# A vision tower with experts on one core: seven tiles embedded in the first turns, logits spread out, norm statistics on ScalarE

## The chip, the cores and the metric

One NeuronCore of one Trainium2 chip. The metric is the device time of one execution in microseconds; lower is better. The change is compared with the kernel before by the medians of several executions.

## What is computed

32 images of 3 x 96 x 96 become 36 patches each plus a class token: 1184 rows of 256 numbers, in ten tiles of 128 rows (the last has 32). Then:

```python
h = embed(x)                                  # patches @ W.T + b, class token, positions
x0 = layernorm(h)                             # no weights
xn = layernorm(x0) * w1 + b1
q, k, v = xn @ Wq.T, xn @ Wk.T, xn @ Wv.T     # + biases; 16 heads of 16
q, k = elu(q) + 1, elu(k) + 1
attn = per token, over its heads: q (k v) / (q sum(k))
x1 = x0 + attn @ Wo.T + bo
x2 = layernorm(x1) * w2 + b2
h2 = h + x1 + gelu(x2 @ Wfc.T + bfc) @ Wproj.T + bproj
y = layernorm(h2)                             # no weights
scores = softmax(y @ gate.T)                  # 16 experts, each takes its 148 best rows
out = h2 + shared_mlp(y) + sum over the chosen experts of weight * expert(y)
```

All in float32; the attention works within one token, so tiles are independent until the experts choose their rows.

## The kernel before

Five engines run written-out streams that meet by semaphores; nothing schedules them but the order of the code. The front half is a software pipeline of ten turns (`turn(t)` on TensorE, ScalarE and VectorE, a loop of the same shape on GpSimd). In turn t the tiles stand at different stages: tile t has its attention products made on VectorE, tile t-1 is summed by transposes (`sum_values`), projected and normed to x2, tile t-2 goes through the hidden layer (`mlp`, `project_mlp`), tile t-3 is normed to y and turned, tile t+1 is projected to q, k, v, tile t+2 is normed (x0, xh) and turned, and tile t+3 is embedded (`embed`, seven matmuls) at the end of the turn.

- Norms: VectorE makes mean and variance of 256 numbers with two instructions (`moments`, L777 and L780), three times a tile: `a_moments` of h, `c_moments` of x1, `f_moments` of h2. GpSimd turns them into 1/sqrt and a shift (`inverse_root`, `shift_of`), ScalarE applies these (`norm_a`, `scale_xh`, `norm_c`, `norm_f`; L550, L570). xh is x0 with its second norm's factor.
- ScalarE also copies PSUM to SBUF (`copy_h`, `copy_v`, `turn_attn`, `turn_y`), and has Exp in the same turn as Gelu, which have different tables (ACT_TABLE_LOAD). `load_exp` loads the table of Exp early with a tiny activation on `warm`.
- Embedding has one PSUM bank and two patch buffers: TensorE waits until the last tile's copy was made, SyncE asks for the patches of tile n as soon as tile n-2 was embedded. Small matmuls without use (`keep_busy`) fill TensorE's first waits.
- Behind the last turns a tail finishes tiles 8 and 9. The seven first of 20 blocks of the shared MLP's first layer are made in and behind turns 8 and 9 (`EARLY`), the others and the second layer are a filler between the steps of the routing (`fill`). The logits of tiles 0 to 8 come at once before the last tile's y is turned:

```python
turn_y(s9.off(-1))
early(5, 6)
pe.wait_ge(yT_made, TILES - 1)
for t in range(TILES - 1):
    logits(t)
turn_y(s9)
```

- Then come softmax, ten rounds of counting that find each expert's threshold (VectorE and TensorE in turn), the slots, and from about 305 us on sixteen experts, which the change does not touch.

## Time and profile before

| | us |
|---|---|
| median of 3 executions | 504.08 (502.46 to 504.34) |
| profiled execution, its own time | 504.55 |
| its span, first to last instruction | 502.8 |
| TensorE busy | 459.9 (91%) |
| VectorE busy | 362.0 (72%) |
| ScalarE busy | 224.4 (45%) |
| GpSimd busy | 152.3 (30%) |
| chain that ended last: PE, DVE, ACT, issue | 66%, 14%, 5%, 5% |

In rows, PE is TensorE (its matmuls; weight loads have rows of their own), DVE VectorE, ACT ScalarE, POOL GpSimd. L followed by a number is a line of the kernel. A bracket at a timeline's row tells how long the engine was idle before it, and what released it. A float32 matmul counts as two. Shares of busy time are averages over all stages: what an engine costs is read in a turn.

### The profile page before, as it was taken

The page shows a single profiled execution, that of the slowest core. Times are in us where ns is not written, and L with a number is a line of the kernel's source. Part 1 is how long each engine was busy: PE and PEld are TensorE (multiplying, and loading weights), DVE is VectorE, ACT ScalarE, POOL GpSimd, SP SyncE. Part 2 cuts the span into 40 slices and gives each one's busy share as a digit, 9 for nine tenths or more (in the row PEclk, how much of TensorE's full clock was granted, in tenths as well). Part 3 has the DMA queues.
Part 4 walks back from the last instruction along what each step waited for, and adds up shares of the span by engine and source line. Part 5 has one row for each costly group of instructions (what it writes and reads, how often), then busy time and mean ns, then how long its engine had stood idle before and what let it go on. Part 6 is the DMA issues. An engine that isn't in the chain of part 4 may idle for free.

```text
span 502.8 us, 10363 instructions
## 1 busy us (share of the span) xinstructions
PE 459.9 (91%) x3853; PEld 404.9 (81%) x3853; DVE 362.0 (72%) x674; ACT 224.4 (45%) x527; POOL 152.3 (30%) x252
## 2 busy tenths in 40 slices
PE   6987899999999998999798499899999999999990
PEld 3555778888888887888677388899999999999990
DVE  1289898999999999621488687588877667777720
ACT  1432264664664752334341005445555566666520
POOL 1312033142142122121000052164433747446322
PEclk9999699999999999999789969989999999999996
DMA  7965101101000000000000016978878888888421
GB/s 246 370 231 252 35 1 34 43 1 45 10 13 0 12 12 10 1 10 23 7 1 0 0 29 220 372 275 303 295 286 284 307 324 329 319 319 324 113 26 13
DMA packets 17348, 69.12 MB, mean 137 GB/s; under 512 B 4338, under 2 KB 10399, under 8 KB 12834
## 3 DMA queue, kind: packets, MB, share of 16 engines
q1 hardware_dynamic: 12130, 61.96, 32.9%
q0 software_dynamic: 4608, 5.41, 5.3%
q10 hardware_dynamic: 576, 1.29, 0.7%
q8 instruction: 22, 0.36, 0.3%
q14 instruction: 12, 0.10, 0.1%
HBM read 63.32 MB, written 5.33 MB: 137 GB/s over the span
## 4 chain that ended last, share of the span: by engine, by line
PE 66%; DVE 14%; ACT 5%; issue 5%; DMA 3%; POOL 1%; DVEq 0%; ACTq 0%; POOLq 0%
PE bank L1407 18%; PE bank L1418 13%; PE bank L1181 5%; PE bank L1210 5%; PE bank L1195 5%; PE bank L1125 4%; PE bank L1315 4%; DVE qkt L795 4%; DMA wex_s<-in_wex 3%; DVE scratch L961 2%; PE bank L1140 2%; DVE scratch L790 2%; PE bank L1169 1%; DVE late L809 1%; PE bank L1429 1%
## 5 line engine op out<-in xcount | busy, mean ns | idle before, releaser
L1418 PE MATMUL bank<-scratch,wex_s 128*128 128x148 f32 x512 | 78.4, 297 | 0.2 <-DVE scratch L1053 0.2
L503 POOL DMA_INDIRECT out_rows<-scratch,slot_s x32 | 51.8, 1619 | 83.9 <-DMA out_rows<-scratch,slot_s 61.5
L492 POOL DMA_INDIRECT xg<-token_rows,slot_g x32 | 44.5, 1391 | 81.2 <-DVE slot_g L1026 72.3
L1418 PEld LDWEIGHTS bank<-scratch,wex_s 128*128 128x128 f32 x512 | 68.2, 192 | 0.5 <-DVE scratch L1053 0.5
L420 POOL TENSOR_SCALAR tmp<-mv 128x1 f32<-128x1 f32 x30 | 6.7, 222 | 166.6 <-DVE mv L780 166.6
L724 ACT ACTIVATE scratch<-bank 128x296 f32<-128x296 f32 x64 | 26.6, 416 | 67.2 <-PE bank L1407 67.2
L1407 PE MATMUL bank<-scratch,wsh_s 128*128 128x148 f16 x512 | 53.7, 230 | 0.0
L1407 PE MATMUL bank<-scratch,wfc_s 128*128 128x148 f16 x512 | 52.6, 228 | 0.0
L1407 PE MATMUL bank<-scratch,wproj_s 128*128 128x148 f16 x256 | 50.6, 227 | 0.0
L944 DVE SCALAR_TENSOR_TENSOR wproj_s<-wex_s,wfc_s 128x512 f16<-128x512 f32 x64 | 40.4, 682 | 12.6 <-ACT wfc_s L707 12.6
L1053 DVE SCALAR_TENSOR_TENSOR scratch<-bank,scratch 128x296 f32<-128x296 f32 x64 | 29.4, 460 | 27.0 <-ACT scratch L724 26.9
L790 DVE TENSOR_TENSOR scratch<-qk 128x2048 f32<-128x2048 f32 x20 | 45.5, 2291 | 4.2 <-PE bank L1195 3.9
L795 DVE TENSOR_REDUCE qkt<-scratch 128x128 f32<-128x2048 f32 x20 | 45.1, 2257 | 0.3 <-issue 0.3
L1407 PEld LDWEIGHTS bank<-scratch,wsh_s 128*128 128x128 f16 x512 | 42.9, 99 | 1.2
L1407 PEld LDWEIGHTS bank<-scratch,wfc_s 128*128 128x128 f16 x512 | 42.1, 98 | 1.5 <-issue 0.4
L1169 PEld LDWEIGHTS bank<-x2T,wfc_s 128*128 128x128 f32 x320 | 37.2, 192 | 4.4 <-issue 3.3
L1407 PE MATMUL bank<-scratch,wtok_s 128*128 128x148 f16 x192 | 40.0, 230 | 0.0
L1210 PE MATMUL bank<-yT,wsh_s 128*128 128x256 f32 (+1 forms) x160 | 38.3, 396 | 0.0
L707 ACT ACTIVATE wfc_s<-wex_s 128x512 f16<-128x512 f32 x64 | 36.5, 632 | 3.6 <-DMA wex_s<-in_wex 3.6
L1169 PE MATMUL bank<-x2T,wfc_s 128*128 128x128 f32 x320 | 37.5, 276 | 0.7 <-ACT x2T L574 0.7
L1181 PE MATMUL bank<-wproj_s,hidT 128*128 128x256 f32 x160 | 36.9, 384 | 0.8
L944 DVE SCALAR_TENSOR_TENSOR wtok_s<-wex_s,wsh_s 128x512 f16<-128x512 f32 x48 | 30.2, 682 | 8.9 <-ACT wsh_s L707 8.9
(162 smaller groups left out, 908.0 us busy)
## 6 DMA issues: line engine op xcount, KB each, us to landing
wex_s<-in_wex SPq DMA_DIRECT2D x16, 2048.0 KB, 7.9
wex_s<-in_wex SPq DMA_DIRECT2D x16, 1024.0 KB, 8.4
patch_s<-in_patches SPq DMA_DIRECT2D x10, 384.0 KB
token_rows<-y_s SPq DMA_DIRECT2D x10, 128.0 KB, 1.8
out_rows<-h_all SPq DMA_DIRECT2D x5, 256.0 KB, 6.5
wfc_s<-in_wfc SPq DMA_DIRECT2D x1, 1024.0 KB, 5.2
wproj_s<-in_wproj SPq DMA_DIRECT2D x1, 1024.0 KB, 7.2
wsh_s<-in_wsh SPq DMA_DIRECT2D x1, 1024.0 KB, 8.9
```

The lines of the kernel that those rows point to most:

```text
L492: gp.indirect_dma_start(xg[b][:], None, rows, bass.IndirectOffsetOnAxis(slot_g[b][:], 0))\
L503: gp.indirect_dma_start(out, bass.IndirectOffsetOnAxis(slot_s[b][:], 0), eo[b], None, compute_op=ALU.add).then_inc(scattered, 16)
L707: act.activation(w16(s.par, 0, n), wex_s[s.par][:, n * n16:(n + 1) * n16], ACT.Copy, scale=SPLIT).then_inc(whi_made, 1)
L790: ve.tensor_tensor(dst.rearrange("p (h j d) -> p h j d", h=HH, j=H), q, k, ALU.mult).then_inc(v_chain, 1)
L795: ve.tensor_reduce(qkt[:, g * HH:(g + 1) * HH, :], src.rearrange("p (h j d) -> p h j d", h=HH, j=H), AX, ALU.add).then_inc(v_chain, 1)
L944: ve.scalar_tensor_tensor(w16(s.par, 1, n), wex_s[s.par][:, n * n16:(n + 1) * n16], SPLIT, w16(s.par, 0, n), ALU.mult, ALU.subtract).then_ ...
L1053: ve.scalar_tensor_tensor(hexT[:, 2 * p:2 * p + 2, :].rearrange("p m c -> p (m c)"), ps_up[p % 2][:, 0:2 * C], 1 / SPLIT ** 2, gel[p % 2], ...
L1169: last = pe.matmul(ps_fc[m // 4][:, (m % 4) * P:(m % 4 + 1) * P], wfc_s[:, k, m * P:(m + 1) * P], x2T[:, k, :], start=(k == 0), stop=(k == ...
L1181: last = pe.matmul(ps_proj[:, 0:D], hidT[:, m, :], wproj_s[:, m, :], start=False, stop=(m == MC - 1))
L1210: last = pe.matmul(ps_shared(j)[:, x * SPAN:x * SPAN + width(lo)], wsh_s[:, k, x * SH + m * P:x * SH + (m + 1) * P], yT[:, k, lo:lo + widt ...
L1407: last = pe.matmul(dst[p % 2][:, x * C:(x + 1) * C], w16(s.par, a, piece)[:, lo:lo + P], x16[s.par][b][:, k, :], start=(n == 0), stop=(n = ...
L1418: last = pe.matmul(ps_down[k][:, 0:C], wex_s[s.par][:, lo:lo + P], hexT[:, m, :], start=(m == 0), stop=(m == MC - 1))
```

## The change

1. The tiles are embedded earlier: tiles 2 and 3 ahead of turn 0 (in the place of 14 idle matmuls), 4, 5, 6 in turn 0, 7 and 8 in turn 1, 9 in turn 2. The odd ones use bank 7, the others bank 0. The loads of patches move ahead of those of the hidden layer, the shared MLP and the experts; the stores of y move behind all loads.
2. The logits of tile t-4 come in turn t, the last three in the tail. One shared block less is made early (six).
3. `moments` goes. The copy of the embedding and the two additions give the row's sum beside their result (`accum_out`; the additions become scalar_tensor_tensor). ScalarE makes minus the mean of it (`less`), then a Square with that as its bias, whose own running sum is 256 times the variance (`spread`). GpSimd scales this sum, and needs one instruction less for the shift.

```diff
-        ps_tok, ps_tr, ps_qk, ps_v, ps_o = bank[0], bank[1], bank[2], bank[3], bank[4]
+        ps_tr, ps_qk, ps_v, ps_o = bank[1], bank[2], bank[3], bank[4]
         ps_fc, ps_proj = (bank[5], bank[6]), bank[7]
...
+        def ps_tok(t):
+
+            return bank[7 if t % 2 and t < TILES - 1 else 0]
...
-        stats = sb("stats", [P, 3, 6])
-        mv = sb("mv", [P, 3, 2])
-        tmp = sb("tmp", [P, 9])
+        total, less, spread = sb("total", [P, 3, TILES]), sb("less", [P, 3, TILES]), sb("spread", [P, 3, TILES])
+        beside = sb("beside", [P, D])
+        tmp = sb("tmp", [P, 6])
...
-        EARLY = 7
+        EARLY = 6
...
-            sp.dma_start(wo_s[:], wo).then_inc(w_in["o"], 16)
-            sp.dma_start(wfc_s[:], wfc).then_inc(w_in["fc"], 16)
-            sp.dma_start(wproj_s[:], wproj).then_inc(w_in["proj"], 16)
...
             next_patch(Step(0, 2))
+            sp.dma_start(wo_s[:], wo).then_inc(w_in["o"], 16)
+            next_patch(Step(0, 3))
+            sp.dma_start(wfc_s[:], wfc).then_inc(w_in["fc"], 16)
+            sp.dma_start(wproj_s[:], wproj).then_inc(w_in["proj"], 16)
+            for t in range(4, TILES):
+                next_patch(Step(0, t))
             sp.dma_start(gate_s[:], gate).then_inc(w_in["moe"], 16)
             sp.dma_start(wsh_s[:], wsh).then_inc(w_in["moe"], 16)
             sp.dma_start(wsd_s[:], wsd).then_inc(w_in["moe"], 16)
-            next_patch(Step(0, 3))
-            next_patch(Step(0, 4))
             load_gu(Step(0, 0), 0)
             load_dn(Step(0, 0), 0)
             load_gu(Step(0, 1), 1)
-            for t in range(5, TILES):
-                next_patch(Step(0, t))
-                if t >= 8:
-                    store_y(Step(0, t - 8))
-            for t in range(TILES - 8, TILES):
+            for t in range(TILES):
                 store_y(Step(0, t))
...
-            def inverse_root(k, var, base_count):
+            def inverse_root(k, squares, base_count):
 
                 gp.sem_inc(p_passed, 1)
-                gp.tensor_scalar(tmp[:, k:k + 1], var, EPS, None, ALU.add).then_inc(p_chain, 1)
+                gp.tensor_scalar(tmp[:, k:k + 1], squares, 1 / D, EPS, ALU.mult, ALU.add).then_inc(p_chain, 1)
                 gp.wait_ge(p_chain, base_count(1))
                 return gp.tensor_tensor(rstd[:, k:k + 1], tmp[:, k:k + 1], nhalf[:], ALU.pow)
 
-            def shift_of(k, at):
+            def shift_of(k, t, at):
 
                 gp.wait_ge(p_chain, at(2))
-                gp.tensor_tensor(tmp[:, 6 + k:7 + k], rstd[:, k:k + 1], mv[:, k, 0:1], ALU.mult).then_inc(p_chain, 1)
-                gp.wait_ge(p_chain, at(3))
-                return gp.tensor_tensor(shift[:, k:k + 1], tmp[:, 6 + k:7 + k], minus[:], ALU.mult)
+                return gp.tensor_tensor(shift[:, k:k + 1], rstd[:, k:k + 1], less[:, k, t:t + 1], ALU.mult)
...
+            def squares(k, t, src, done):
+
+                nonlocal means
+                means += 1
+                act.sem_inc(a_passed, 1)
+                act.activation(less[:, k, t:t + 1], total[:, k, t:t + 1], ACT.Copy, scale=-1 / D).then_inc(mean_made, 1)
+                act.wait_ge(mean_made, means)
+                act.sem_inc(a_passed, 1)
+                act.activation(beside[:], src, ACT.Square, bias=less[:, k, t:t + 1],
+                               accum_out=spread[:, k, t:t + 1]).then_inc(done, 1)
+
             def copy_h(s):
                 act.wait_ge(tok_done, s.times(1, 1))
-                act.activation(h_all[:, s.n, :], ps_tok[:, 0:D], ACT.Copy).then_inc(h_copied, 1)
+                act.activation(h_all[:, s.n, :], ps_tok(s.n)[:, 0:D], ACT.Copy, accum_out=total[:, 0, s.n:s.n + 1]).then_inc(h_copied, 1)
+                act.wait_ge(h_copied, s.times(1, 1))
+                squares(0, s.n, h_all[:, s.n, :], a_stats)
+
+            def squares_c(s):
+                act.wait_ge(x1_made, s.times(1, 1))
+                squares(1, s.n, x_all[:, s.n, :], c_stats)
+
+            def squares_f(s):
+                act.wait_ge(h2_made, s.times(1, 1))
+                squares(2, s.n, h_all[:, s.n, :], f_stats)
...
+            copy_h(Step(0, 2))
             turn_xn(Step(0, 1))
+            copy_h(Step(0, 3))
...
-            def turn(t, blocks=()):
+            def turn(t, soon=(), late_on=(), blocks=()):
                 s = Step(0, t)
                 if t + 1 < TILES:
                     load_exp()
...
                     copy_v(s.off(1))
                     negate_qk(s.off(1))
                     exp_qk(s.off(1))
+                if t >= 3:
+                    squares_f(s.off(-3))
                 if t >= 2:
                     gelu(s.off(-2))
+                if t >= 1:
+                    squares_c(s.off(-1))
                 if t + 2 < TILES:
                     norm_a(s.off(2))
                     scale_xh(s.off(2))
+                for n in soon:
+                    copy_h(Step(0, n))
                 if t >= 3:
                     norm_f(s.off(-3), t >= 5)
                 if t >= 1:
...
                     turn_xn(s.off(2))
                 if t >= 3:
                     turn_y(s.off(-3))
-                if t + 3 < TILES:
-                    copy_h(s.off(3))
+                for n in late_on:
+                    copy_h(Step(0, n))
                 for j in blocks:
                     gelu_shared(j)
 
-            for t in range(TILES - 2):
+            turn(0, (4,), (5, 6))
+            turn(1, (7,), (8,))
+            turn(2, (), (9,))
+            for t in range(3, TILES - 2):
                 turn(t)
-            turn(TILES - 2, (0,))
-            turn(TILES - 1, (1, 2))
+            turn(TILES - 2, blocks=(0,))
+            turn(TILES - 1, blocks=(1, 2))
...
             gelu(s9.off(-1))
+            squares_f(s9.off(-2))
             turn_attn(s9)
             gelu_shared(3)
             norm_f(s9.off(-2))
+            squares_c(s9)
             norm_c(s9)
             turn_x2(s9)
             turn_y(s9.off(-2))
+            squares_f(s9.off(-1))
             gelu_shared(4)
             gelu(s9)
             norm_f(s9.off(-1))
             turn_y(s9.off(-1))
+            squares_f(s9)
             gelu_shared(5)
             norm_f(s9)
-            gelu_shared(6)
             load_exp()
             turn_y(s9)
...
-            def a_moments(s, at):
-                ve.wait_ge(h_copied, s.times(1, 1))
-                ve.wait_ge(a_rstd, s.times(1, 0))
-                moments(0, h_all[:, s.n, :], at, a_stats)
-
-            def c_moments(s, at):
+            def add_attn(s):
                 ve.wait_ge(o_done, s.times(1, 1))
                 ve.wait_ge(x0_made, s.times(1, 1))
-                ve.tensor_tensor(x_all[:, s.n, :], ps_o[:, 0:D], x_all[:, s.n, :], ALU.add).then_inc(x1_made, 1)
-                ve.wait_ge(x1_made, s.times(1, 1))
-                ve.wait_ge(c_rstd, s.times(1, 0))
-                moments(1, x_all[:, s.n, :], at, c_stats)
-
-            def f_moments(s, at):
+                ve.scalar_tensor_tensor(x_all[:, s.n, :], ps_o[:, 0:D], 1.0, x_all[:, s.n, :], ALU.mult, ALU.add,
+                                        accum_out=total[:, 1, s.n:s.n + 1]).then_inc(x1_made, 1)
+
+            def add_mlp(s):
                 ve.wait_ge(proj_done, s.times(1, 1))
                 ve.wait_ge(hx_made, s.times(1, 1))
-                ve.tensor_tensor(h_all[:, s.n, :], ps_proj[:, 0:D], hx[:], ALU.add).then_inc(h2_made, 1)
-                ve.wait_ge(h2_made, s.times(1, 1))
-                ve.wait_ge(f_rstd, s.times(1, 0))
-                moments(2, h_all[:, s.n, :], at, f_stats)
+                ve.scalar_tensor_tensor(h_all[:, s.n, :], ps_proj[:, 0:D], 1.0, hx[:], ALU.mult, ALU.add,
+                                        accum_out=total[:, 2, s.n:s.n + 1]).then_inc(h2_made, 1)
 
             def combine(s):
...
-                if t + 2 < TILES:
-                    a_moments(s.off(2), after(1))
                 if t >= 3:
-                    f_moments(s.off(-3), after(1))
+                    add_mlp(s.off(-3))
                 qk_sum(s, 1, mine, product1)
                 after(1)
                 if t >= 1:
-                    c_moments(s.off(-1), after(1))
+                    add_attn(s.off(-1))
                 for j in blocks:
...
+            def embed(t):
+
+                s = Step(0, t)
+                pe.wait_ge(patch_in[s.par], s.half * 32 + 32)
+                if t >= 2:
+                    pe.wait_ge(h_copied, t - 1 if t < TILES - 1 else t)
+                pe.matmul(ps_tok(t)[:, 0:D], sel_s[s.par][:], base_s[:], start=True, stop=False)
+                for k in range(TKC):
+                    last = pe.matmul(ps_tok(t)[:, 0:D], patch_s[s.par][:, k, :], wtok_s[:, k, :], start=False, stop=(k == TKC - 1))
+                last.then_inc(tok_done, 1)
...
-            keep_busy(10)
+            embed(2)
             turn_xh(Step(0, 1))
-            keep_busy(4)
-
-            embed(Step(0, 2))
-
-            def turn(t, blocks=()):
+            embed(3)
+
+            def turn(t, soon=(), late_on=(), blocks=()):
...
+                for n in soon:
+                    embed(n)
                 if t >= 1:
                     turn_x2(s.off(-1))
                 if t + 2 < TILES:
                     turn_xh(s.off(2))
                 if t >= 3:
                     turn_y(s.off(-3))
-                if t + 3 < TILES:
-                    embed(s.off(3))
+                if t >= 4:
+                    logits(t - 4)
+                for n in late_on:
...
-            turn(0)
+            turn(0, (4,), (5, 6))
             pe.wait_ge(w_in["o"], 16)
-            turn(1)
+            turn(1, (7,), (8,))
             pe.wait_ge(w_in["fc"], 16)
             pe.wait_ge(w_in["proj"], 16)
-            for t in range(2, TILES - 2):
+            turn(2, (), (9,))
+            turn(3)
+            pe.wait_ge(w_in["moe"], 48)
+            pe.wait_ge(h_copied, TILES)
+            for t in range(4, TILES - 2):
                 turn(t)
-            pe.wait_ge(w_in["moe"], 48)
-            turn(TILES - 2, (0,))
-            turn(TILES - 1, (1, 2))
+            turn(TILES - 2, blocks=(0,))
+            turn(TILES - 1, blocks=(1, 2))
...
             project_mlp(s9.off(-1))
+            logits(TILES - 4)
             early(4)
             turn_x2(s9)
             turn_y(s9.off(-2))
...
             project_mlp(s9)
             pe.wait_ge(yT_made, TILES - 2)
             turn_y(s9.off(-1))
-            early(5, 6)
+            logits(TILES - 3)
+            early(5)
             pe.wait_ge(yT_made, TILES - 1)
-            for t in range(TILES - 1):
-                logits(t)
+            logits(TILES - 2)
             turn_y(s9)
             pe.wait_ge(yT_made, TILES)
             logits(TILES - 1).then_inc(logits_done, 1)
```

Three places show how the order moves. ScalarE, a whole turn in the middle, before (`warm` starts the turn; neg and expo are the Exp of tile t+1, hidT the Gelu of tile t-2):

```order
L597 ACTIVATE attnT<-bank 128x256
L593 ACTIVATE vx<-bank 128x256
L585 ACTIVATE neg<-bank 128x512
L589 ACTIVATE expo<-neg 128x512
L608 ACT_TABLE_LOAD
L608 ACTIVATE hidT<-bank,colc 128x128 x8
L550 ACTIVATE x_all<-h_all,shift,rstd 128x256
L570 ACTIVATE xh<-x_all,rstd 128x256
L550 ACTIVATE y_s<-h_all,shift,rstd 128x256
L550 ACTIVATE x<-x_all,shift,rstd 128x256
L574 ACTIVATE x2T<-bank,colc 128x128 x2
L574 ACTIVATE xnT<-bank,colc 128x128 x2
```

and now, the same place:

```order
L615 ACTIVATE vx<-bank 128x256
L607 ACTIVATE neg<-bank 128x512
L611 ACTIVATE expo<-neg 128x512
L550 ACTIVATE less<-total 128x1
L553 ACTIVATE beside,spread<-h_all,less 128x256
L630 ACT_TABLE_LOAD
L630 ACTIVATE hidT<-bank,colc 128x128 x8
L550 ACTIVATE less<-total 128x1
L553 ACTIVATE beside,spread<-x_all,less 128x256
L572 ACTIVATE x_all<-h_all,shift,rstd 128x256
L592 ACTIVATE xh<-x_all,rstd 128x256
L572 ACTIVATE y_s<-h_all,shift,rstd 128x256
```

One pair of less and beside (the squares of h2) stands between expo and the Gelu table load, a second (those of x1) between hidT and the norms.

TensorE up to the first sum of values (L1195), before from the transpose of xh of tile 1 (L1110):

```order
L1110 MATMUL bank<-kst,xh 128x128 x2
L1232 MATMUL bank<-ones_b 128x512 x4
L1123 MATMUL bank<-base_s,sel_s 128x256
L1125 MATMUL bank<-wtok_s,patch_s 128x256 x6
L1114 MATMUL bank<-bias_s,ones_b 128x256
L1147 MATMUL bank<-wqkv_s,xnT 128x256 x2
L1114 MATMUL bank<-bias_s,ones_b 128x512
L1140 MATMUL bank<-wqkv_s,xnT 128x512 x2
L1110 MATMUL bank<-kst,xh 128x128 x2
L1123 MATMUL bank<-base_s,sel_s 128x256
L1125 MATMUL bank<-wtok_s,patch_s 128x256 x6
L1195 MATMUL bank<-kst,scratch 128x128 x16
```

and now from the projections of tile 1:

```order
L1126 MATMUL bank<-bias_s,ones_b 128x256
L1157 MATMUL bank<-wqkv_s,xnT 128x256 x2
L1126 MATMUL bank<-bias_s,ones_b 128x512
L1150 MATMUL bank<-wqkv_s,xnT 128x512 x2
L1134 MATMUL bank<-base_s,sel_s 128x256
L1136 MATMUL bank<-wtok_s,patch_s 128x256 x6
L1122 MATMUL bank<-kst,xh 128x128 x2
L1134 MATMUL bank<-base_s,sel_s 128x256
L1136 MATMUL bank<-wtok_s,patch_s 128x256 x6
L1134 MATMUL bank<-base_s,sel_s 128x256
L1136 MATMUL bank<-wtok_s,patch_s 128x256 x6
L1205 MATMUL bank<-kst,scratch 128x128 x16
```

The embeddings of tiles 2 and 3 now stand ahead of the first row. Before the first sum of values the tiles up to 6 are embedded, where it was up to 3.

TensorE's tail, from the last projection of the hidden layer (L1181), before:

```order
L1181 MATMUL bank<-wproj_s,hidT 128x256 x8
L1110 MATMUL bank<-kst,y_s 128x128 x2
L1210 MATMUL bank<-yT,wsh_s 128x256 x8
L1219 MATMUL bank<-gate_s,yT 128x16 x18
L1110 MATMUL bank<-kst,y_s 128x128 x2
L1219 MATMUL bank<-gate_s,yT 128x16 x2
```

and now:

```order
L1191 MATMUL bank<-wproj_s,hidT 128x256 x8
L1122 MATMUL bank<-kst,y_s 128x128 x2
L1229 MATMUL bank<-gate_s,yT 128x16 x2
L1220 MATMUL bank<-yT,wsh_s 128x256 x4
L1229 MATMUL bank<-gate_s,yT 128x16 x2
L1122 MATMUL bank<-kst,y_s 128x128 x2
L1229 MATMUL bank<-gate_s,yT 128x16 x2
```

The 18 logit matmuls before the last turned y have become 2 and 2, and one shared block of four is gone from between.

## Rows read from the trace of the kernel before

**Rows 1.** Chain that ended last: start (us), length (us), engine and line.

```profile
78.37 3.49 PE bank L1195 x32
...
174.54 2.28 DVE scratch L790
...
192.34 2.29 DVE scratch L790
```

**Rows 2.** Timeline, turn 5: start, busy us, engine, line, operation, out<-in.

```profile
106.04 1.28 ACT L608 ACT_TABLE_LOAD   x1
...
108.53 3.72 PE L1181 MATMUL bank<-wproj_s,hidT 128*128 128x256 f32 x16
...
109.35 0.64 ACT L550 ACTIVATE x_all<-h_all,shift,rstd 128x256 f32<-128x256 f32 x1
...
111.01 0.58 ACT L550 ACTIVATE x<-x_all,shift,rstd 128x256 f32<-128x256 f32 x1
...
112.09 0.38 PE L1110 MATMUL bank<-kst,x 128*128 128x128 f32 x2
```

**Rows 3.** Timeline of TensorE, turn 7 (the first that embeds nothing).

```profile
154.10 1.91 PE L1195 MATMUL bank<-kst,scratch 128*128 128x128 f32 x16
...
169.01 0.38 PE L1110 MATMUL bank<-kst,x 128*128 128x128 f32 x2
...
170.34 1.94 PE L1195 MATMUL bank<-kst,scratch 128*128 128x128 f32 x16 [0.51 <-issue]
```

**Rows 4.** Timeline of VectorE, statistics of turn 7; idle time before in brackets.

```profile
158.26 0.42 DVE L777 BATCH_NORM_STATS2 stats<-h_all 128x6 f32<-128x256 f32 x1
...
158.93 0.43 DVE L827 TENSOR_TENSOR h_all<-bank,hx 128x256 f32<-128x256 f32 x1
159.53 0.43 DVE L777 BATCH_NORM_STATS2 stats<-h_all 128x6 f32<-128x256 f32 x1 [0.17 <-DVE h_all L827]
```

**Rows 5.** Groups by line and form, 0 to 270 us: busy us, mean ns of one.

```profile
L570 ACT ACTIVATE xh<-x_all,rstd 128x256 f32<-128x256 f32 x10 | 5.1, 508 | 2.3 <-POOL rstd L422 1.4
...
L535 ACT ACTIVATE warm<-warm 1x1 f32<-1x1 f32 x11 | 2.2, 198 | 0.1
...
L961 DVE DVE_READ_ACCUMULATOR scratch<-scratch,way 128x1 f32 x7 | 0.6, 83 | 0.0
```

**Rows 6.** Timeline, first turns, all engines, 0 to 60 us.

```profile
25.70 2.86 PE L1125 MATMUL bank<-wtok_s,patch_s 128*128 128x256 f32 x12
...
33.93 0.44 PE L1110 MATMUL bank<-kst,xh 128*128 128x128 f32 x2 [2.46 <-ACT xh L570]
...
34.92 4.54 PE L1125 MATMUL bank<-wtok_s,patch_s 128*128 128x256 f32 x12
...
39.30 1.91 PE L1195 MATMUL bank<-kst,scratch 128*128 128x128 f32 x16
...
51.70 0.69 PE L1110 MATMUL bank<-kst,x 128*128 128x128 f32 x2 [4.85 <-ACT x L550]
...
59.17 2.19 PE L1195 MATMUL bank<-kst,scratch 128*128 128x128 f32 x16
```

**Rows 7.** Timeline, the last turns and the tail, all engines, 188 to 244 us.

```profile
201.73 0.44 PE L1110 MATMUL bank<-kst,x 128*128 128x128 f32 x2 [1.45 <-ACT x L550]
...
230.13 3.62 PE L1210 MATMUL bank<-yT,wsh_s 128*128 128x256 f32 x16
...
233.24 0.60 ACT L550 ACTIVATE y_s<-h_all,shift,rstd 128x256 f32<-128x256 f32 x1 [0.80 <-POOL shift L429]
...
233.59 4.38 PE L1219 MATMUL bank<-gate_s,yT 128*128 128x16 f32 x36
...
238.94 1.03 PE L1219 MATMUL bank<-gate_s,yT 128*128 128x16 f32 x4 [0.47 <-ACT yT L614]
```

**Rows 8.** Timeline, TensorE at the stage that finds the slots.

```profile
288.60 1.40 PE L1366 MATMUL bank<-late 128*74 128x4 bf16 x20 [5.24 <-DVE late L1013]
```

**Rows 9.** Page: granted TensorE clock in tenths, 40 slices of 12.57 us.

```profile
PEclk9999699999999999999789969989999999999996
```

More of the change, by code:

```diff
@@ L451, in norm_f @@
                 gp.wait_ge(y_made, s.times(1, 0))
[L452 to L453 removed]
+                inverse_root(2, spread[:, 2, s.n:s.n + 1], at).then_inc(p_chain, 1)
+                shift_of(2, s.n, at).then_inc(f_rstd, 1)
             def sum_hx(s):
@@ L468, in after @@
                 return lambda k: base + k
-            norm_a(Step(0, 0), after(6))
-            norm_a(Step(0, 1), after(6))
+            norm_a(Step(0, 0), after(5))
+            norm_a(Step(0, 1), after(5))
             for t in range(TILES + 3):
@@ L474, in _ @@
                 if t + 2 < TILES:
-                    norm_a(s.off(2), after(6))
+                    norm_a(s.off(2), after(5))
                 if t >= 3:
-                    norm_f(s.off(-3), after(3))
+                    norm_f(s.off(-3), after(2))
                 if 2 <= t < TILES + 2:
@@ L480, in _ @@
                 if 1 <= t <= TILES:
-                    norm_c(s.off(-1), after(3))
+                    norm_c(s.off(-1), after(2))
             def gather(s, first):
@@ L846, in shared_hidden @@
                                  gel_sh[:, (j % 2) * SPAN:(j % 2) * SPAN + n], ALU.mult).then_inc(shid_made, 1)
-            chain = 2
+            chain = 0
             def after(n):
@@ L900, in _ @@
             shared_hidden(1)
-            f_moments(s9.off(-2), after(1))
+            add_mlp(s9.off(-2))
             shared_hidden(2)
-            c_moments(s9, after(1))
+            add_attn(s9)
             shared_hidden(3)
-            f_moments(s9.off(-1), after(1))
+            add_mlp(s9.off(-1))
             shared_hidden(4)
-            f_moments(s9, after(1))
+            add_mlp(s9)
             shared_hidden(5)
-            shared_hidden(6)
             def link(ins):
@@ L1114, in add_bias @@
                 pe.matmul(dst[:, 0:n], ones_b[0:BP, :], bias_s[:, lo:lo + n], start=True, stop=False)
-            def embed(s, part=None):
-                cut = TKC // 2
-                if part != 1:
-                    pe.wait_ge(patch_in[s.par], s.half * 32 + 32)
-                    if not (isinstance(s.n, int) and s.n == 0):
-                        pe.wait_ge(h_copied, s.times(1, 0))
-                    pe.matmul(ps_tok[:, 0:D], sel_s[s.par][:], base_s[:], start=True, stop=False)
-                for k in range(cut if part == 1 else 0, cut if part == 0 else TKC):
-                    last = pe.matmul(ps_tok[:, 0:D], patch_s[s.par][:, k, :], wtok_s[:, k, :], start=False, stop=(k == TKC - 1))
-                if part != 0:
-                    last.then_inc(tok_done, 1)
+            def embed(t):
[7 more added lines that the diff above has]
+                last.then_inc(tok_done, 1)
             def turn_xh(s):
@@ L1236, in _ @@
             pe.wait_ge(w_in["tok"], 32)
-            embed(Step(0, 0))
-            embed(Step(0, 1))
+            embed(0)
+            embed(1)
             pe.wait_ge(w_in["consts"], 32)
```

30 lines of the change are left out of this document (10 added, 20 removed).

## The prediction

> **What bounds the kernel now.** I read the chain of waits first. From 78 to 154 us it is a TensorE chain: the transposes that sum one tile's values start at 78.37 and, four turns later, at 154.10, so a turn takes 18.93 us [rows 1, 3]. In turns 8 and 9 the chain runs through VectorE, with 17.80 us from product to product [rows 1]. The change acts on exactly these two engines. The timeline of one TensorE-bound turn shows what else lies close: after the exponentials ScalarE loads the Gelu table at 106.04, TensorE can start projecting the hidden layer only at 108.53, and the normalised x2 starts at 111.01, lasts 0.58 and is turned by TensorE at 112.09, some 0.44 us later than it could have been [rows 2]. The reader should see that ScalarE is only half busy and still has almost no slack at two places in a turn. Turn 7, which embeds nothing, shows TensorE's turn without an embedding: 154.10 to 170.34, 16.24 us. Its last piece, from turning x2 (169.01) to the next sum, is 1.33 us, which waits for ScalarE to write x2T [rows 3]. The last view is the tail, where 36 narrow logit matmuls hold TensorE for 4.38 us between the last tile's norm and its transpose [rows 7].
>
> **What changes, part by part.**
>
> *VectorE.* Each pair of statistics instructions goes: 158.26 to 158.93, 0.67 us, and behind the two additions also a 0.17 us wait for their own result [rows 4]. That is 3 x 0.67 + 2 x 0.17 = 2.35 us a turn. The additions become forms with a running sum; the only accumulator read in the trace costs 0.08 [rows 5], so 0.16 comes back. VectorE's full turn, 18.5 (17.80 for turn 8, which lacks one pair, plus 0.67), falls to about 16.3. So VectorE leaves the bound. By itself this gains nothing in the turns that TensorE bounds.
>
> *ScalarE.* Each pair comes back there as a mean (one element per partition) and a Square over 256. The nearest rows are 0.198 for the tiny activation and 0.508 for a 256-wide one with one per-partition operand [rows 5]. With two gaps of 0.03 that is 0.77. Reading the sum out is in no row of ScalarE: lower bound nothing (0.77, or 0.71 if the gaps overlap), upper bound another full activation (1.3). I take 0.1, near VectorE's 0.08, so s = 0.87 for one pair.
>  Square is not used before, so a table could have to be loaded for it. A load is 1.28 us [rows 2]; two more a turn would cost six turns some 15 us. The order of instructions has 16 loads before and 16 after, so I add none. [...]
>
> *TensorE, steady turns.* Tiles 5 to 9 are no longer embedded in turns 2 to 6 (only tile 9 stays, in turn 2). The turn falls from 18.93 to 16.24, and the 0.49 us of logits that is added (4.38/9, [rows 7]) fits into the 1.33 us at its end: turn xh and turn y take 0.4 of that. But the f pair now stands between the exponentials and the Gelu table load, on the path to 108.53, at full price: +0.87. The c pair stands between Gelu and the x2 norm: +0.87 less the 0.44 of slack, +0.43. Its other path, through GpSimd, is the same length or shorter: the three norms ahead of x2 take 1.66 (109.35 to 111.01). New turn: 16.24 + 0.87 + 0.43 = 17.54. From the sum of tile 2 to that of tile 7 there are five: 87.7 against 92.0 (78.37 to 170.34). **-4.3.**
>
> *First turns.* Seven embeddings (2 and 3 ahead, 4 to 6 in turn 0, 7 and 8 in turn 1, 9 in turn 2) at 2.86 x 7/6 = 3.3 us each at full clock [rows 6] replace four. Copying tile 1 now also squares it, ahead of the first xnT: +0.6. The count, in full clock: tile 0's projections end at about 21.9; embedding 2 to 25.2, xh of tile 1 to 25.6, embedding 3 to 28.9, projections of tile 1 (2.9) to 31.8, embeddings 4, 5, 6 and a turned xh to 42.1, so tile 0 is summed 2.8 us later than now (39.30). From a sum to x2 a turn takes 14.9 (154.10 to 169.01, [rows 3]), 7.5 of it the hidden layer, which turn 1 lacks: 42.1 + 7.4 = 49.5, embedding 7 to 52.8. Today TensorE then sits idle for 4.85 us at 51.70 for x2, and sums tile 1 at 59.17 with a slow clock [rows 6]. After the change x2 comes at about 54.9, since it queues on ScalarE behind the copy and squares of tile 7: 2.1 us idle, two transposes, embedding 8, and tile 1 is summed at 58.6 (VectorE has it ready at about 57). Turn 2: 58.6 + 14.9 + 0.4 of stall + 0.4 + 3.3 = 77.6, against 78.37. The patches have two buffers; each is asked for two embeddings ahead, and weights are moved behind them, so I charge no wait for data. [...] -0.8 + 1.7 = **+0.9.**
>
> *Turn 8.* It embeds nothing before either, and gains an obstacle: 16.24 - 1.33 + 0.4 (two transposes) + 0.5 (logits) + 1.8 (a shared block, half of 3.62, [rows 7]) = 17.65, plus 0.87 + 0.3 for the pairs = 18.8 on TensorE, against 17.8 on VectorE now. **+1.0.**
>
> *Turn 9.* TensorE waited 1.45 us for x2 [rows 7]. VectorE reaches that addition 0.84 sooner, the squares cost 0.2 more than the statistics, GpSimd has one instruction less (0.27). **-0.8.**
>
> *Tail.* Logits 5 and 6 come before the last projection: **+1.0.** After it, the last norm now starts at about 233.2, as at 233.24 today (squares 0.1 to 0.2 dearer, GpSimd one instruction less). Today TensorE turns it only at 238 (233.59 + 4.38), after one more shared block and nine logits; now it is free at 232.9 (230.13 + 1.8 + 2 x 0.49). What is late next is ScalarE: norm to 233.8, table load and warm-up to 235.3, yT to 235.7, then the last logits, 0.5 to 1.0, to 236.5, against 239.97 [rows 7]. **-3.5.**
>
> *Middle.* The seventh shared block (1.8 us) moves into the filler behind the routing rounds. There TensorE is idle for 5.24 us [rows 8] and six more filler matmuls go into that gap, so the block is hidden; without that cover it costs 1.8. Behind this gap the slice from 289 to 302 us shows a granted clock of 6 tenths [rows 9], so most of four filler groups of 1.8 us ran twice as long. A gap of 2.6 instead of 5.24 should shorten that. Bounds: nothing, and 3.8 us; I take **-1.0.** The expert phase is not touched.
>
> Sum: -4.3 + 0.9 + 1.0 - 0.8 + 1.0 - 3.5 - 1.0 = -6.7. The profiled execution took 504.55 and so gives 497.85; it lies 0.47 over the median shown (504.08), and against that median I forecast **497.4 us**.
>
> **The rivals.**
> 1. *ScalarE becomes the bound (slower).* The place is the f pair between exp and Gelu and the c pair behind Gelu. Every 0.1 us of s costs twice in six turns and once or twice at both ends, 1.4 us. [...] At s = 1.6 the time is 497.4 + 7.3 x 1.4 = 507.6. For it: no accumulating activation in the trace. Against it: the cheap 0.08 of VectorE's. Chance 0.13. [...]
> 2. *The opening gives it back (no change).* The half clock lasts as after the 4.85 us gap (+2.3), a second dip comes in turn 0 (+1.7) and a patch is 1 us late: 502.4. For it: the clock fell at both places today [rows 6, 9]. Against: TensorE has more work there, not less. Chance 0.13.
> 3. *The pairs are hidden and VectorE bounds every turn.* Five turns at 16.34 in place of 17.54 and turn 8 at 17.7: 6.0 + 1.1 less, 490.3. For it: ScalarE is half idle. Against it: [rows 2] show no slack at the hidden layer. Chance 0.08.
>
> **How the numbers follow.** My forecast has 0.66 and spreads from 494 (s = 0.71, no dip in the clock) to 502 (s = 1.1, a longer dip). Within 0.5% is about what a measurement of this kernel can tell from no change, that is 501.6 to 506.6. Faster by more than that: 0.62 of my own case, 0.04 of the second rival, 0.08 of the third, 0.74. Within: 0.04 + 0.09 + 0.02 of the first, 0.15. Slower: the rest of the first rival, 0.11. The range 492.5 to 505 leaves out most of rivals 1 and 3, 0.19 together.
>
> **What would show it.** In the profile after: turns 3 to 7 of 17.5 us between sums of values; a gap of about 1 us on TensorE before the hidden projection and of 0.4 before x2 is turned; Square near 0.5 and the pair near 0.87; VectorE with over 1 us idle a turn; tile 2 summed between 77 and 80; scores starting 3.5 us sooner behind the last projection; a shorter half-clock stretch in the slot stage. I am wrong if the pair takes over 1.3 us (then slower), if turns come out at 16.3 (then rival 3), or if tile 2 is summed after 82 (rival 2).

## Result: 8.6% slower, where 1.3% faster was forecast

| | before | changed |
|---|---|---|
| median of 4 executions, us | 503.27 (500.52 to 504.34) | 545.78 (544.86 to 547.46) |
| ratio, 95% interval | | 1.086 (1.082 to 1.090) |
| span of the profiled execution | 502.8 | 543.2 |
| TensorE, VectorE, ScalarE, GpSimd busy | 459.9, 362.0, 224.4, 152.3 | 468.9, 345.6, 248.2, 204.1 |
| mean granted TensorE clock | 0.953 | 0.935 |

GpSimd is the surprise: one instruction less a norm, and 52 us more busy. From the page of the changed kernel: the clock row, to compare with [rows 9], the chain's shares, and a group of two-operand scalar instructions on 128 single numbers.

```profile
PEclk9999798978989788798998988998999999999996
...
PE 58%; POOL 10%; DVE 5%; ACT 4%; issue 4%; DMA 2%; POOLq 0%; ACTq 0%; DVEq 0%
...
L421 POOL TENSOR_SCALAR tmp<-spread 128x1 f32<-128x1 f32 x30 | 24.9, 829 | 167.7 <-ACT beside L553 163.1
```

Before, GpSimd had 1% of the chain (the chain of waits that ended last), and now 10%. The mean of 829 ns hides two kinds. The view of one line gives minimum, median and maximum in ns; first the 1/sqrt of the changed kernel, then the same line before.

```profile
L423 POOL TENSOR_TENSOR rstd<-tmp,nhalf x40: 549/550/2670, 13.8 to 279.6; 128x1 f32<-128x1 f32 x40
```

```profile
L422 POOL TENSOR_TENSOR rstd<-tmp,nhalf x40: 567/568/576, 13.6 to 232.0; 128x1 f32<-128x1 f32 x40
```

The median is as it was; some take five times as long. Timeline of one turn of the changed kernel, GpSimd, VectorE and what waits (start, busy us; idle time before in brackets):

```profile
122.05 0.21 POOL L421 TENSOR_SCALAR tmp<-spread 128x1 f32<-128x1 f32 x1 [12.04 <-ACT beside L553]
122.31 2.29 DVE L835 TENSOR_TENSOR scratch<-qkt,vx 128x2048 f32<-128x2048 f32 x1
...
122.34 2.67 POOL L423 TENSOR_TENSOR rstd<-tmp,nhalf 128x1 f32<-128x1 f32 x1
...
124.52 2.29 DVE L835 TENSOR_TENSOR late<-qkt,vx 128x2048 f32<-128x2048 f32 x1
125.09 1.77 POOL L428 TENSOR_TENSOR shift<-rstd,less 128x1 f32<-128x1 f32 x1
...
125.95 0.18 ACT L553 ACTIVATION_READ_ACCUMULATOR beside<-x_all,less 128x1 f32 x1
...
127.44 2.29 DVE L816 TENSOR_TENSOR scratch<-qk 128x2048 f32<-128x2048 f32 x1
127.62 2.15 POOL L421 TENSOR_SCALAR tmp<-spread 128x1 f32<-128x1 f32 x1
...
129.86 0.55 POOL L423 TENSOR_TENSOR rstd<-tmp,nhalf 128x1 f32<-128x1 f32 x1
130.49 0.19 POOL L428 TENSOR_TENSOR shift<-rstd,less 128x1 f32<-128x1 f32 x1
...
130.80 0.60 ACT L572 ACTIVATE x<-x_all,shift,rstd 128x256 f32<-128x256 f32 x1 [3.07 <-POOL shift L428]
...
131.45 0.67 PE L1122 MATMUL bank<-kst,x 128*128 128x128 f32 x2 [3.40 <-ACT x L572]
```

The second L421 starts 0.18 us behind a product of 2.29 us and ends at 129.77, 0.04 behind the product's end at 129.73; L423 (122.34) ends 0.41 behind its product, about its own length. So a tiny instruction that meets a product seems to do its work only when the product has ended: in the trace of the changed kernel 29 GpSimd instructions start while such a product runs, and every one of them ends behind it: by 0.05 us those that otherwise take 0.19, by 0.41 those that take 0.55, by 0.59 those that take 0.73. Both operands of these products (L816, L835) lie in SBUF. The norm of x2 is late twice over. GpSimd takes y's norm first, which meets two products (L423 at 122.34, L428 at 125.09); it comes to x2's, whose sum was read out at 126.13, only at 127.62, and there meets a third. TensorE is idle for 3.40 us, 3.88 in the turns around it. Before, the same stage of a turn fell beside a reduction, which has one operand:

```profile
106.71 2.25 DVE L795 TENSOR_REDUCE qkt<-scratch 128x128 f32<-128x2048 f32 x1
107.23 0.22 POOL L420 TENSOR_SCALAR tmp<-mv 128x1 f32<-128x1 f32 x1
107.53 0.57 POOL L422 TENSOR_TENSOR rstd<-tmp,nhalf 128x1 f32<-128x1 f32 x1
...
108.44 0.19 POOL L429 TENSOR_TENSOR shift<-tmp,minus 128x1 f32<-128x1 f32 x1
```

VectorE's statistics stood right behind its additions and ahead of the reductions, so GpSimd's turn came beside the reductions. ScalarE's squares stand behind the exponentials and behind Gelu, and the products are what VectorE does then. TensorE's marks, from the first transposes that sum a tile to the next one's (timeline of the changed kernel; sums of tiles 2, 7 and 9):

```profile
88.39 1.91 PE L1205 MATMUL bank<-kst,scratch 128*128 128x128 f32 x16
...
202.41 3.65 PE L1205 MATMUL bank<-kst,scratch 128*128 128x128 f32 x16
...
258.06 1.91 PE L1205 MATMUL bank<-kst,scratch 128*128 128x128 f32 x16
```

| us | before | changed | experiment 3 | experiment 4 |
|---|---|---|---|---|
| up to the sum of tile 0 | 39.30 | 42.31 | 41.78 | 42.67 |
| tile 0 to 2 | 38.90 | 46.08 | 36.08 | 35.87 |
| tile 2 to 7, five turns | 92.14 | 114.02 | 87.56 | 83.64 |
| tile 7 to 8 | 17.10 | 26.69 | 18.76 | 18.04 |
| tile 8 to 9 | 23.53 | 28.96 | 22.62 | 22.44 |
| tile 9 to the end | 291.8 | 285.1 | 286.6 | 283.7 |

Every stretch with a norm in it lost, the five steady turns most (21.9 of 40.4 us). The 3.0 us up to the first sum are mostly the earlier embeddings, for which 2.8 were forecast; the part behind the last sum won 6.7, as forecast in kind. The sum at 202.41 took 3.65 us at a granted clock of 0.50, behind a wait of 3.71 us; the one at 88.39 took 1.91 at 1.00.

### The profile page after: what moved, and what is told of

The parts are those of the page before. It is cut to its first block, busy times and chain, and to the rows that moved or that the text cites. A ratio compares the mean times of both kernels' runs of the same rounds, so it can differ in the third digit from the quotient of the medians.

```text
span 543.2 us, 10364 instructions
## 1 busy us (share of the span) xinstructions
PE 468.9 (86%) x3839; PEld 413.6 (76%) x3839; DVE 345.6 (64%) x634; ACT 248.2 (46%) x627; POOL 204.1 (38%) x221
## 4 chain that ended last, share of the span: by engine, by line
PE 58%; POOL 10%; DVE 5%; ACT 4%; issue 4%; DMA 2%; POOLq 0%; ACTq 0%; DVEq 0%
PE bank L1423 17%; PE bank L1434 12%; PE bank L1205 7%; PE bank L1220 5%; POOL tmp L421 3%; PE bank L1331 3%; POOL rstd L423 3%; POOL shift L428 3%; DMA wex_s<-in_wex 2%; PE bank L1179 2%; PE bank L1150 2%; DVE scratch L973 2%; PE bank L1122 2%; PE bank L1168 1%; PE bank L1191 1%
## 5 line engine op out<-in xcount | busy, mean ns | idle before, releaser
L421 POOL TENSOR_SCALAR tmp<-spread 128x1 f32<-128x1 f32 x30 | 24.9, 829 | 167.7 <-ACT beside L553 163.1
L816 DVE TENSOR_TENSOR scratch<-qk 128x2048 f32<-128x2048 f32 x20 | 45.8, 2294 | 62.2 <-PE bank L1205 61.9
L491 POOL DMA_INDIRECT xg<-token_rows,slot_g x32 | 47.3, 1479 | 74.2 <-DVE slot_g L1038 65.4
L956 DVE SCALAR_TENSOR_TENSOR wproj_s<-wex_s,wfc_s 128x512 f16<-128x512 f32 x64 | 40.4, 683 | 12.4 <-ACT wfc_s L741 12.4
L1220 PE MATMUL bank<-yT,wsh_s 128*128 128x256 f32 (+1 forms) x160 | 40.1, 408 | 0.0
L1191 PEld LDWEIGHTS bank<-wproj_s,hidT 128*128 128x128 f32 x160 | 29.6, 190 | 11.5 <-ACT hidT L630 7.7
```

Of the source, the lines that this page charges most:

```text
L421: gp.tensor_scalar(tmp[:, k:k + 1], squares, 1 / D, EPS, ALU.mult, ALU.add).then_inc(p_chain, 1)
L491: gp.indirect_dma_start(xg[b][:], None, rows, bass.IndirectOffsetOnAxis(slot_g[b][:], 0))\
L816: ve.tensor_tensor(dst.rearrange("p (h j d) -> p h j d", h=HH, j=H), q, k, ALU.mult).then_inc(v_chain, 1)
L956: ve.scalar_tensor_tensor(w16(s.par, 1, n), wex_s[s.par][:, n * n16:(n + 1) * n16], SPLIT, w16(s.par, 0, n), ALU.mult, ALU.subtract).then_ ...
L1191: last = pe.matmul(ps_proj[:, 0:D], hidT[:, m, :], wproj_s[:, m, :], start=False, stop=(m == MC - 1))
L1220: last = pe.matmul(ps_shared(j)[:, x * SPAN:x * SPAN + width(lo)], wsh_s[:, k, x * SH + m * P:x * SH + (m + 1) * P], yT[:, k, lo:lo + widt ...
```

## Experiments

The theory to test is that GpSimd waits for VectorE's two-operand products. In the expectations of experiments 1 to 8 this theory is P. In that of experiment 9 it is L, and P is its rival. Each kernel was measured beside the kernel before.

**1. Parts 1 and 2 of the change alone.** Statistics back on VectorE, embedding and logits as changed.

```diff
-                if t >= 3:
-                    squares_f(s.off(-3))
...
-                if t >= 1:
-                    squares_c(s.off(-1))
...
-                    add_attn(s.off(-1))
+                    c_moments(s.off(-1), after(1))
```

> The changed kernel with means and variances back on VectorE (the two statistics instructions), early embeddings and spread logits kept. Theory P (GpSimd's small norm instructions wait for VectorE's two-operand products, because the squares on ScalarE come so late in the turn that the norm falls beside those products): GpSimd's instructions stay at 0.19 to 0.57 us, turns are VectorE-bound at about 18.5 us, total 498 to 502. Rival O (the embeddings in the first turns are the cause): stays above 530. Rival S (the longer chain on ScalarE itself, pairs of 0.93 us): also 498 to 502, so this run only parts O from the others.

497.18 us, ratio 0.988 (0.985 to 0.991), just under the 498 expected. The embedding and the logits are no cause of the loss; they bring 1.2%. The statistics cost the changed kernel 545.78 - 497.18 = 48.6 us.

**2. Part 3 alone.** The kernel before, with the statistics on ScalarE at the places of the change.

> The kernel before with only the statistics moved to ScalarE; embeddings and logits where they were. Theory P: GpSimd instructions of 2 us and more again, turns of 24 to 27 us (the 22.8 to 23.6 of the changed kernel, and the embedding of 2.9 to 3.3 at its end), total 550 to 570. Rival O: near 504 plus little, under 512. Rival S: 1.4 us a turn more than before, 512 to 518.

561.85 us, ratio 1.119 (1.115 to 1.123): the loss needs nothing but part 3. Turns are about 27 us.

**3. Products that read one operand.** This leaves out the multiplications by k and by v. Shown is the product of q and k; the one with v is changed in the same way.

```diff
-                ve.tensor_tensor(dst.rearrange("p (h j d) -> p h j d", h=HH, j=H), q, k, ALU.mult).then_inc(v_chain, 1)
+                ve.tensor_reduce(dst.rearrange("p (h j d) -> p h j d", h=HH, j=H), q.unsqueeze(4), AX, ALU.add).then_inc(v_chain, 1)
```

> The changed kernel with VectorE's four products of 128x2048 a turn replaced by reductions over one element, which read one operand from SBUF and write as much; it leaves out the multiplications by k and by v. If their length stays near 2.2 us, only the second SBUF operand goes. Theory P: GpSimd's instructions return to 0.19 to 0.57 us, turns to about 17.6, total 494 to 502. Rival S and rival O: unchanged, 540 to 548.

496.69 us, ratio 0.988 (0.986 to 0.991). Timeline of its turn, at the places shown above:

```profile
108.34 2.28 DVE L835 TENSOR_REDUCE late<-qkt 128x2048 f32<-128x2048 f32 x1
...
109.70 0.19 POOL L421 TENSOR_SCALAR tmp<-spread 128x1 f32<-128x1 f32 x1 [2.31 <-ACT beside L553]
109.97 0.55 POOL L423 TENSOR_TENSOR rstd<-tmp,nhalf 128x1 f32<-128x1 f32 x1
110.60 0.19 POOL L428 TENSOR_TENSOR shift<-rstd,less 128x1 f32<-128x1 f32 x1
...
111.62 0.44 PE L1122 MATMUL bank<-kst,x 128*128 128x128 f32 x2 [0.21 <-ACT x L572]
```

VectorE is busy as long as in the changed kernel at the same places, all waits of the program are there, and 49 us are gone. From the start of L423 to that of L428 it is 0.63 us, where the changed kernel took 2.75 (122.34 to 125.09).

This run takes away the multiplication together with the second SBUF operand. The changed kernel's own trace tells the two apart, in two multiplications of 128x256: the one of `qkt` and `rden`, both in SBUF, and the one of the shared MLP, which has one operand in PSUM (`bank`). GpSimd's 1/sqrt takes 0.77 beside the first and its usual 0.55 beside the second. The other meetings in that trace are alike: all seven GpSimd instructions that start beside the product of `qkt` and `rden` (0.42 us) end behind it, by 0.05 or 0.41, and the eight that start beside a two-operand instruction that reads `bank` (L840, L852, L860) take 0.19, 0.55 and 0.73 as ever. So it is the second SBUF operand, not the multiplication.

```profile
144.30 0.42 DVE L827 TENSOR_TENSOR qkt<-qkt,rden 128x256 f32<-128x256 f32 x1
144.36 0.77 POOL L423 TENSOR_TENSOR rstd<-tmp,nhalf 128x1 f32<-128x1 f32 x1
```

```profile
271.54 0.42 DVE L860 TENSOR_TENSOR wtok_s<-bank,gel_sh 128x256 f32<-128x256 f32 x1 [4.16 <-ACT gel_sh L659]
271.73 0.55 POOL L423 TENSOR_TENSOR rstd<-tmp,nhalf 128x1 f32<-128x1 f32 x1
```

**4. Both pairs of squares ahead of the exponentials.** They then stand behind the copy of v, and GpSimd works beside the reductions again.

```diff
                     copy_v(s.off(1))
+                if t >= 3:
+                    squares_f(s.off(-3))
+                if t >= 1:
+                    squares_c(s.off(-1))
+                if t + 1 < TILES:
                     negate_qk(s.off(1))
                     exp_qk(s.off(1))
-                if t >= 3:
-                    squares_f(s.off(-3))
                 if t >= 2:
                     gelu(s.off(-2))
-                if t >= 1:
-                    squares_c(s.off(-1))
```

> The changed kernel with the two pairs of squares moved on ScalarE: both stand behind the copy of v and ahead of the exponentials' first step, in place of behind them and behind Gelu. The norms on GpSimd then fall beside VectorE's reductions. Theory P: GpSimd's c and f chains at 0.19 to 0.57 us an instruction, turns of about 17 us (16.24, plus about 0.7 by which the exponentials and Gelu start later), total 490 to 497, faster than before. Rival S: ScalarE has as much to do and the exponentials are later, so still slower than before, over 515.

489.69 us, ratio 0.972 (0.966 to 0.978): faster than both kernels and just under the 490 expected, with turns of 16.73. In its timeline the reductions start at 116.62 and 119.16, and the norms of y and x2 lie beside them:

```profile
119.11 0.19 POOL L428 TENSOR_TENSOR shift<-rstd,less 128x1 f32<-128x1 f32 x1
...
119.16 2.28 DVE L822 TENSOR_REDUCE qkt<-scratch 128x128 f32<-128x2048 f32 x1
...
120.50 0.19 POOL L421 TENSOR_SCALAR tmp<-spread 128x1 f32<-128x1 f32 x1 [0.53 <-ACT beside L553]
120.78 0.55 POOL L423 TENSOR_TENSOR rstd<-tmp,nhalf 128x1 f32<-128x1 f32 x1
...
123.93 3.72 PE L1192 MATMUL bank<-wproj_s,hidT 128*128 128x256 f32 x16 [0.58 <-ACT hidT L630]
...
128.00 2.22 POOL L428 TENSOR_TENSOR shift<-rstd,less 128x1 f32<-128x1 f32 x1
```

The last row shows that the norm of the next tile's x0 still meets a product, where nobody waits for it: ScalarE reads the result only in the next turn.

**5 and 6. Only one pair early**: x1's (5, `squares_c`), h2's (6, `squares_f`).

> The changed kernel with only the c pair (x1) ahead of the exponentials; the f pair (h2) stays behind them. GpSimd takes the norms in a fixed order, f, then hx, then c. Theory P: the f norm still starts just as VectorE's products start (in the changed kernel at 122.05 against 122.31), and the c norm is queued behind it, so c gains nothing from its early squares: over 530. Were it only a matter of where c's own squares stand, it would come near the 490 of the run with both early.

> The changed kernel with only the f pair early; the c pair stays behind Gelu. Theory P: the f norm and hx run beside the reductions, and only the c norm's three instructions meet the last product; x2 is 1 to 4 us late in each turn. Between the two: 505 to 530.

535.29 us, ratio 1.068 (1.064 to 1.073), and 540.77, ratio 1.078 (1.076 to 1.080). The first is as expected, the second is a miss: I thought that a GpSimd queue cleared of y's norm would let x2's through in time. Its timeline shows why not:

```profile
146.63 2.28 DVE L836 TENSOR_TENSOR late<-qkt,vx 128x2048 f32<-128x2048 f32 x1
...
147.15 1.81 POOL L421 TENSOR_SCALAR tmp<-spread 128x1 f32<-128x1 f32 x1 [5.50 <-ACT beside L553]
...
149.55 2.29 DVE L817 TENSOR_TENSOR scratch<-qk 128x2048 f32<-128x2048 f32 x1
149.67 2.22 POOL L428 TENSOR_TENSOR shift<-rstd,less 128x1 f32<-128x1 f32 x1
...
152.66 0.69 PE L1123 MATMUL bank<-kst,x 128*128 128x128 f32 x2 [3.80 <-ACT x L572]
```

The queue is free for 5.50 us, yet x2's own instructions meet two products, the second by 0.12 us. The wait is as long as in the changed kernel. In 5 y's norm meets two products (L423 takes 2.67, L428 1.76) and holds x2's in the queue, and then x2's own L421 meets a third (2.16). Either pair left late is enough to lose the turn.

**7. Idle matmuls in the wait for x2.** 14 of them, in turns 1 to 7.

```diff
+                if 1 <= t < TILES - 2:
+                    keep_busy(14)
                 if t >= 1:
                     turn_x2(s.off(-1))
```

> The changed kernel with 14 idle bf16 matmuls (3.0 us at full clock) ahead of turning x2 in turns 1 to 7, where TensorE is idle for 3.5 to 4.6 us. It takes away no wait. If part of the loss is the clock that falls after each such gap (sums of values of 5.2 to 5.9 us in place of 3.5), the granted clock stays near 1.0 there and the total falls by 7 to 15 us, to 531 to 539. If the clock has no share, it stays at 546.

528.85 us, ratio 1.056 (1.052 to 1.059), under the 531 to 539 expected: the clock's share is 17 us, 8.1 of it in the five steady turns. Windows over the five steady turns, changed kernel and this one (busy us of each engine, granted clock):

```profile
88.39:202.41 114.02, 90.23 (x528) 77.51 (x526) 79.26 (x70) 61.83 (x154) 50.97 (x63) 0.90 0.02 7
```

```profile
84.40:190.30 105.90, 95.84 (x598) 74.75 (x596) 79.26 (x70) 61.32 (x153) 51.56 (x63) 1.00 0.02 7
```

So a steady turn of 22.80 us is 17.51 as in experiment 3, plus 3.67 of waiting (idle 3.88 against 0.21), plus 1.62 at a lower granted clock (22.80 - 105.90/5; 0.90 over the five turns, and 1.00 here).

**8. Part 3 alone, squares early.** Experiment 2 with the order of 4.

> The kernel before with the statistics moved to ScalarE, both pairs early; embeddings and logits where they were. Theory P: no long GpSimd instruction on the path; turns TensorE-bound at 18.97 plus about 0.5 by which Gelu is later, so 503 to 509, about the same as before: VectorE's relief alone is worth nothing while TensorE still embeds in each turn.

502.31 us, ratio 1.001 (0.998 to 1.003), just under the 503 expected; steady turns take 19.46, and 18.97 before. Moving the statistics to ScalarE, with the squares early, is worth nothing while TensorE also embeds in each turn, and 497.18 - 489.69 = 7.5 us once it does not. (Single executions of experiment 4 spread over 8 us, so this difference is rough.)

**9. The changed kernel with each product in four.** Shown is the product with v; that of q and k is cut in the same way.

```diff
-                ve.tensor_tensor(dst.rearrange("p (j h e) -> p j h e", j=H, h=HH), a, v, ALU.mult).then_inc(prod_made, 1)
+                for part in range(4):
+                    lo, hi = part * H // 4, (part + 1) * H // 4
...
+                    last = ve.tensor_tensor(dst.rearrange("p (j h e) -> p j h e", j=H, h=HH)[:, lo:hi], a, v, ALU.mult)
+                last.then_inc(prod_made, 1)
```

> The changed kernel with each of VectorE's 128x2048 products written as four instructions of 128x512 (about 0.6 us each in place of 2.29), everything else as it is. Theory L (a GpSimd instruction that meets a two-operand product waits until that one VectorE instruction ends): the wait is then at most 0.6 us for each, no GpSimd instruction of 128x1 takes over 1.3 us, and the x2 norm comes 1.6 to 3.7 us earlier in a turn. VectorE pays about 0.2 us per product for the extra instructions, some 0.8 a turn. Turns of 20 to 21.5 us in place of 23, the time 515 to 535 (I take 525). Rival P (the products take GpSimd's access for as long as their stream lasts, however it is cut): GpSimd's instructions still end only after the fourth quarter, at 2.2 us and more, and the time is 545 to 555.

501.57 us, ratio 0.998 (0.995 to 1.002), 44 us faster than the changed kernel and well under my 515 to 535. Timeline:

```profile
112.23 2.50 DVE L840 TENSOR_TENSOR late<-qkt,vx 128x512 f32<-128x512 f32 x4
...
112.62 0.33 POOL L421 TENSOR_SCALAR tmp<-spread 128x1 f32<-128x1 f32 x1 [2.08 <-ACT beside L553]
...
113.04 0.87 POOL L423 TENSOR_TENSOR rstd<-tmp,nhalf 128x1 f32<-128x1 f32 x1
...
113.99 0.19 POOL L428 TENSOR_TENSOR shift<-rstd,less 128x1 f32<-128x1 f32 x1
...
114.96 0.44 PE L1128 MATMUL bank<-kst,x 128*128 128x128 f32 x2 [0.62 <-ACT x L572]
```

The arithmetic is the same, but GpSimd gets in between two quarters: L421 takes 0.33 and L423 0.87. So the wait lasts about as long as one VectorE instruction (a quarter takes 0.68), not as long as the products. I had added up more waits than there are. In this turn y's norm meets no product at all (its L428 starts at 109.23, the first quarter at 109.27), TensorE waits 0.62 us for x2, and turns take 17.9 in place of the 20 to 21.5 expected. The largest L421 is 1827 ns, above the 1.3 us that I had named and longer than two quarters: GpSimd does not get in at every boundary.

**10. Experiment 4 with the products in four.**

> The version with both pairs of squares ahead of the exponentials (489.7 us), with the products in quarters as well: what the cut itself costs where no GpSimd instruction on the path meets a product. VectorE's turn grows from about 16.3 by some 0.8 to 17.1 and passes TensorE's 16.7, so 0 to 0.4 us a turn over nine turns: 490 to 495. If it is below 489 the norms of x0, which still meet products there, were on the path after all.

494.04 us, ratio 0.984 (0.978 to 0.989), as expected. The cut costs some 4 us against the 489.69 of experiment 4 where nothing on the path meets a product, but the single executions of the two overlap (492.91 to 498.51, 486.45 to 494.37). In the profiles a steady turn takes 16.94 in place of 16.73, 0.2 us more.

## Why the prediction was wrong

The step that failed is one sentence in "TensorE, steady turns": "Its other path, through GpSimd, is the same length or shorter: the three norms ahead of x2 take 1.66". The 1.66 us are ScalarE's three activations ahead of x2, and the step holds only if GpSimd has x2's norm ready within them. It was ready before, where GpSimd's four instructions took 1.40 (107.23 to 108.63), and it is in experiment 3, where ScalarE comes from the sum's read-out to x in 1.50 (109.48 to 110.98). In the changed kernel this path through GpSimd takes 4.67 in the turn shown (126.13 to 130.80), and in a steady turn TensorE waits up to 3.88 for x2, where 0.4 was forecast. The sentence gave GpSimd's instructions the length that they have beside reductions, and the change moves them beside products. The trace of before shows no norm beside a product, so the price there was unknown, and it should have been bounded from the rows at hand: up to a whole product of 2.29 us for an instruction. None of the rivals named GpSimd either. The runs show what such a rival would have needed: 1.09 to 2.78 us for GpSimd instructions that start while such a product runs, 0.19 to 0.73 beside a reduction, and 0.19 to 1.18 beside a quarter of the product, but for the single 1.83. A norm beside the products, worked out with a wait of up to 2.29 us an instruction, would have been the rival on the slower side that decided.

Point by point, where the failed step is out of the way (experiment 3, spans against spans):

- **Pair of squares**: forecast 0.87. Measured 0.19 + 0.51 + 0.19 and gaps, 0.92 up to the next instruction's start (rows below). Reading the sum is an instruction of its own. No additional table load came with Square: 16 loads of 1.28 us before and after. The rival of a dear Square is out. Timeline of the changed kernel, a pair on ScalarE and what follows:

```profile
142.96 0.19 ACT L550 ACTIVATE less<-total 128x1 f32<-128x1 f32 x1
143.26 0.51 ACT L553 ACTIVATE beside<-h_all,less 128x256 f32<-128x256 f32 x1
...
143.68 0.19 ACT L553 ACTIVATION_READ_ACCUMULATOR beside<-h_all,less 128x1 f32 x1
143.88 1.28 ACT L630 ACT_TABLE_LOAD   x1
```

- **Steady turns**: forecast 17.54, measured 17.51. Over five turns that is -4.6, forecast -4.3: the mark of 78.37 that I subtracted from is the chain's, and the timeline has it at 78.20. TensorE waits 0.93 us for the hidden layer, forecast "about 1", and 0.21 for x2, forecast 0.4.
- **First turns**: tile 0 forecast at 42.1, at 41.78; wait for x2 forecast 2.1, 2.10; tile 1 forecast 58.6, 58.74; tile 2 forecast 77.6 without the clock, 77.86. The 1.7 us for the clock are an estimate, the 4.54 less the 2.86 us of the two embeddings in [rows 6], taken over for a wait of 2.1 us; the 2.3 of the second rival are the 4 that the wait of 4.85 us cost before (7.47 us at a granted clock of 0.50, 51.70 to 59.17, and 0.28 in the sum behind it), less these 1.7. No run shows 1.7 for such a wait: behind the 2.10 us of experiment 3 the embedding takes 2.86, and the granted clock from 49 to 111 us is 1.00. So -0.3 in place of +0.9. (The "seven embeddings" of the prediction are eight tiles, and its sum counts all eight.)
- **Turn 8**: forecast 18.8, measured 18.76. Against TensorE's 17.10 before that is +1.7; my +1.0 was measured against VectorE's 17.80, the wrong mark.
- **Turn 9**: -0.8 forecast, -0.9 measured.
- **Tail with logits 5 and 6**: -2.5 forecast. From the last sum to the first spreading transposes of the scores it was 35.33 us (210.97 to 246.30) and is 31.47 (206.80 to 238.27): -3.9.
- **Middle**: -1.0 forecast. The idle time of [rows 8] is 2.66, forecast 2.6; from these transposes of the scores to those of the first gathered rows it was 56.38 us (246.30 to 302.68) and is 54.90 (238.27 to 293.17), -1.5. The expert phase is within 0.1.

The sum is -9.4 between these two spans (502.8 and 493.4), where -6.7 was forecast. In the medians it is -6.3 (502.95 and 496.69); the profiled execution of experiment 3 was the fastest of its four. That 496.69 lies so near to the 497.4 forecast is in part luck: the clock's 1.7 did not come and the tail and the middle won 1.9 more than forecast, while turn 8 lost 0.7 more. Still no term of the sum was off by more than 1.7 us, and the one sentence on GpSimd by 48, since a duration is not a property of an instruction alone.

## What to carry to other kernels

Before a small GpSimd instruction is moved, or anything that it waits for, look up what VectorE does at the new time: a product of two SBUF operands cost it the rest of that instruction here (in the changed kernel 0.19 us became up to 2.31, 0.55 up to 2.67, 0.73 up to 2.78). Place such work beside reductions, or cut the long product where it can't be placed (here that won 44 us, and cost about 0.2 us a turn where nothing met a product). And a mean that hides a maximum of five times the median is worth a look at the line.
